# Halving the scatter of a mixture-of-experts block, with small moves in the steps before it

## The chip, the cores and the metric

One core of one Trainium2 chip. The metric is the device time of one launch in microseconds, the median of several runs. "The profiled execution" is one run recorded by the hardware profiler; its span reaches from the first to the last instruction. TensorE (PE) does the matmuls, VectorE (DVE), ScalarE (ACT) and GpSimd (POOL) the rest, SyncE (SP) and the other engines' queues start transfers.

## The reference

Four sequences of 1024 tokens with 512 channels (4096 tokens in all) go through one block:

```
h = layernorm(x) * (1 + ca) + sa                       # sa, ca, ga, sb, cb, gb from silu(c) @ wmod
x = x + ga * linear_attention(h)                        # relu(q), relu(k), 16 heads of 32, projection
h = layernorm(x) * (1 + cb) + sb
scores = sigmoid(h @ gate_w.T);  idx = top_2(scores + router_bias);  w = normalised scores of idx
routed = sum over the 2 chosen experts e:  w_e * (silu(h @ W1_e) * (h @ W3_e)) @ W2_e       # 8 experts, 352 wide
shared = (silu(h @ sw1) * (h @ sw3)) @ sw2                                                   # 704 wide
x = x + gb * (routed + shared)
```

## The kernel before, in words

Every fp32 operand of a large matmul is split in two fp16 parts, high and low, and a product is three matmuls (`split_matmul`, lines 86 to 88: high by high, high by low, low by high). Each engine runs its own hand-ordered program; semaphores join them. `TILES` is 32 (tiles of 128 tokens), `BT` is 8 tiles a sequence.

**Attention.** One loop over steps s does, for tile s, the layernorm, the projections and the sums of keys and values, and, for tile t = s - 9, `attend`, the output projection and the second layernorm; three tiles later come the router's `logits`. The attention part of a sequence needs that sequence's key-value product `vk` (`vk_high` on ScalarE, then `vk_low` on VectorE). The projection's weights are multiplied by the sequence's gate row on GpSimd (`wp_scale`), then split by ScalarE (`wp_high`) and VectorE (`wp_low`): `wp_turn(s)` says which piece in which step. Its last turn is at s = 32, the piece (3, 3). On GpSimd the order in a step is `shift2`, `deviation`, `add_bias`, `wp_scale`, `o_low`. On ScalarE `wp_high` comes after `vk_high` and before the first loads of expert weights and `activate(0)`.

**Shared expert.** From s = 32 on (TILES), two steps q of it go beside each attention step. A chunk is 256 tokens, 16 chunks of six steps: `up(q)` on TensorE, `activate(q)` and `high(q)` on ScalarE, `multiply(q)` and `low(q)` on VectorE; a chunk later in the order, `down(n)` for two tiles of 128 tokens. The sixth step is only 64 columns wide, so its high and low parts sit in the upper and lower 64 rows of one buffer, and the sixth pass of `down` is a 128-row matmul (line 1244) and a 64-row one (line 1245). `add_shared` adds the result to the output in HBM by an indirect transfer from GpSimd with an add. Meanwhile ScalarE and VectorE split the experts' weights, a piece in nearly every step.

**Routing.** After the attention loop (`TAIL_STEPS` is 24) the last `logits(31)` has to come before step 24: TensorE does it at the end of the loop, ScalarE copies it (`logits_out`), VectorE adds the halves (`sum_logits`), ScalarE waits for stores and for that sum and does the sigmoid. Then VectorE does between its steps `bias_scores` (24), `pick_first` (26), `pick_second` (27), `weigh` (28); TensorE counts ranks at step 30; VectorE does `add_runs`, `place`, `name_slots` (32 to 34), masks in steps 35 to 66, `name_tiles` (68) and `list_tokens` (69). The list names, for each of 71 slot tiles of 128 slots, the token and output row of each slot and the tile's expert. It lies where the last expert's weights will be, so ScalarE waits for it (`listed`) before that expert's first piece, at step 81.

**Expert stage.** For each of 71 slot tiles t: GpSimd gathers 128 rows of 2 KB (`gather`, line 422, six buffers), SyncE turns them by a transposing transfer, TensorE does `e_up(t)` (24 matmuls of 352 columns), VectorE and ScalarE form `a`, TensorE transposes it (`e_turn`, line 1323) and does `e_down(t)` (9 matmuls of 512 columns), and VectorE multiplies by a gate row into `y` (`e_out`, line 861, three buffers). TensorE's order is `e_turn(t-1)`, `e_up(t)`, `e_down(t-1)`; in `e_up` and in `e_down` it first reads the tile's expert number into a register. GpSimd's `scatter(t)` (line 428) adds `y` to the rows of the output in HBM. Since two tiles can hold the same token, and an adding transfer reads and then writes, scatter t waits until scatter t - 1 has landed; `e_out(t)` waits for scatter t - 3, to have its buffer free. GpSimd's order is `scatter(t)`, `gather(t + 7)`.

Of the kernel before, what the change touches and what calls it, by code (L numbers as in the profile page):

```python
# [7 lines left out]
I32 = mybir.dt.int32  # L8
U32 = mybir.dt.uint32
ALU = mybir.AluOpType  # L10
# [3 lines left out]
P = 128  # L14
# [39 lines left out]
PAIR_RING = 4  # L54
TURNS_FROM = TAIL_STEPS + 11
LISTED = 3
# [253 lines left out]
def gpsimd_program(nc, m, pool):  # L310
# [61 lines left out]
    for s in range(-3, TILES + TAIL):  # L372
        t = s - LAG
        if s == 0:
            step(pool.memset(m.ident[:, :], 0.0))
            step(pool.affine_select(out=m.ident[:, :], in_=m.ident[:, :], compare_op=ALU.not_equal, fill=1.0,
                                    base=0, pattern=[[-1, P]], channel_multiplier=1))
        if s == 1:
            step(pool.iota(m.row_no[:, :], [[P, TILES]], base=0, channel_multiplier=1))
        if s == 2:  # L380
            step(pool.memset(m.heads[:, :], VK_SCALE))
            step(pool.affine_select(out=m.heads[:, :], in_=m.heads[:, :], compare_op=ALU.is_ge, fill=0.0,
                                    base=0, pattern=[[-HEAD, 4]], channel_multiplier=1))
            step(pool.affine_select(out=m.heads[:, :], in_=m.heads[:, :], compare_op=ALU.is_ge, fill=0.0,
                                    base=HEAD - 1, pattern=[[HEAD, 4]], channel_multiplier=-1))
            step(pool.tensor_copy(m.head_mask[:, :].rearrange("p (h e) -> p h e", h=4),
                                  m.heads[:, :].unsqueeze(2).to_broadcast([P, 4, HEAD])))
        shift(s + 2)
        shift2(t - 2)
        deviation(s + 3)  # L390
        add_bias(t)
        for b, k in wp_turn(s):
            wp_scale(b, k)
        o_low(t)
        deviation2(t - 1)
        if s >= TILES:
            for q in range(STEPS_PER_SLOT * (s - TILES), STEPS_PER_SLOT * (s - TILES + 1)):
                if add_due(q):
                    add_shared(q // SH_TILES - 1)
# [25 lines left out]
    def scatter(t):  # L425
        pool.wait_ge(m.ey_ready, t + 1)
        at_least(pool, m.scattered, 16 * t)
        pool.indirect_dma_start(m.out, bass.IndirectOffsetOnAxis(ap=m.slot_row[:, t:t + 1], axis=0), m.y[:, t % Y_RING, :], None,  # L428
                                compute_op=ALU.add).then_inc(m.scattered, 16)

# [15 lines left out]
    for t in range(SLOT_TILES):  # L446
        scatter(t)
        gather(t + G_RING + 1)
    pool.wait_ge(m.scattered, 16 * SLOT_TILES)


def vector_program(nc, m, v):
# [342 lines left out]
    def list_tokens():  # L795
# [15 lines left out]
        step(v.tensor_tensor(m.rowf[:, :], m.rowf[:, :], m.tokenf[:, :], ALU.add))  # L811
        v.tensor_copy(m.slot_row[:, :], m.rowf[:, :]).then_inc(m.listed, 1)

    def name_tiles():
# [6 lines left out]

    beside = {TAIL_STEPS: (bias_scores,), TAIL_STEPS + 2: (pick_first,), TAIL_STEPS + 3: (pick_second,), TAIL_STEPS + 4: (weigh,),
              TAIL_STEPS + 8: (add_runs,), TAIL_STEPS + 9: (place,), TAIL_STEPS + 10: (name_slots,), LIST_STEP: (list_tokens,),
              LIST_STEP - 1: (name_tiles,)}
    sum_logits()
    for q in range(TAIL_STEPS, EARLY_STEPS):
# [30 lines left out]
    def e_out(t):  # L857
        v.wait_ge(m.ey_done, t + 1)
        v.wait_ge(m.gate_sum, (B - 1) * (t + 1))
        at_least(v, m.scattered, 16 * (t - Y_RING + 1))  # L860
        v.tensor_tensor(m.y[:, t % Y_RING, :], m.ps_ey[:, 0:C], m.gate_row[t % GW_RING][:, :], ALU.mult).then_inc(m.ey_ready, 1)  # L861
# [13 lines left out]
def scalar_program(nc, m, act):  # L875
# [139 lines left out]
    for s in range(-3, TILES + TAIL):  # L1015
# [42 lines left out]
        for j in m.mod_slots.get(s, ()):  # L1058
            act.wait_ge(m.mod_done, j + 1)
            act.activation(m.mod[:, j * C:(j + 1) * C], m.ps_mod[j], ACT.Copy).then_inc(m.mod_copied, 1)  # L1060
        for b, k in wp_turn(s):
            wp_high(b, k)
        if s == TILES:
            for p in range(W_RING - 1):
                w_load(p)
        if s >= TILES:
# [9 lines left out]
            convert_weights(q + 1)  # L1076
    logits_out(TILES - 1)
    for j in range(X2_RING):
        act.wait_ge(m.x2_stored[j], ring_uses(TILES, j, X2_RING))
    for j in range(2):  # L1080
        act.wait_ge(m.hl2_stored[j], ring_uses(TILES, j, 2))
    for j in range(H2T_RING):
        act.wait_ge(m.h2t_stored[j], ring_uses(TILES, j, H2T_RING))

    act.wait_ge(m.logits_ready, 1)
    act.activation(m.scores[:, :, :], m.logits[:, :, 0:E], ACT.Sigmoid).then_inc(m.scores_ready, 1)
    for q in range(TAIL_STEPS, EARLY_STEPS):
        activate(q)
        high(q - 1)
        if w_turn(q):  # L1090
            w_loads(w_turn(q)[0] + W_RING - 1)
        convert_weights(q)
# [29 lines left out]
def tensor_program(nc, m, pe):  # L1122
# [105 lines left out]
    def down(n):  # L1228
# [12 lines left out]
        for u in range(2):  # L1241
            tok = slice(u * P, (u + 1) * P)
            out = m.ps_sy[u][:, 0:C]
            nc.tensor.matmul(out, m.s_at[:, j, 0, tok], m.sh[:, 0, lo:lo + C], start=False, stop=False, skip_group_check=True)
            nc.tensor.matmul(out, m.s_at[0:SH_HALF, j, 0, tok], m.sh[0:SH_HALF, 1, lo:lo + C], start=False, stop=True, skip_group_check=True).then_inc(m.sy_done, 1)

# [11 lines left out]
    for s in range(TILES + TAIL):  # L1258
# [21 lines left out]
        if s >= TILES:  # L1280
# [3 lines left out]
            project_out(t - 1)  # L1284
        logits(t - 3)

    for q in range(TAIL_STEPS, EARLY_STEPS):
        up(q)
        if q == TAIL_STEPS + 6:
            pe.wait_ge(m.both_ready, 1)  # L1290
            pe.wait_ge(m.r_consts, 5)
            for part, lhs in ((0, m.before), (1, m.ones)):
                nc.tensor.matmul(m.ps_r[:, part, :], lhs[:, :], m.both[:, :, :].rearrange("p t e -> p (t e)"),
                                 start=True, stop=True).then_inc(m.ranks_done, 1)
# [11 lines left out]

    def e_up(t):
        expert = expert_of(t)
        pe.wait_ge(m.xt_loaded[t % G_RING], ring_use(t, G_RING))
# [15 lines left out]

    def e_down(t):
        expert = expert_of(t)
        pe.wait_ge(m.e_at_lo, t + 1)
# [10 lines left out]
    pe.wait_ge(m.consts, CONSTS)  # L1339
    e_up(0)  # L1340
    down(CHUNKS - 1)
    pe.wait_ge(m.a_padded, 1)
    for t in range(1, SLOT_TILES):
        e_turn(t - 1)
        e_up(t)
        if t == 1:
            pe.wait_ge(m.s_t1_done, 2 * CHUNKS)
        e_down(t - 1)
    e_turn(SLOT_TILES - 1)
    e_down(SLOT_TILES - 1)  # L1350


def place_buffers(nc, m):
# [16 lines left out]
    END = nc.sbuf_usable_end  # L1370
    KEPT = FIRST + 6400
    SHARED_AT = KEPT + 2 * SH_COLS * 2
# [9 lines left out]
    m.slot_token = sb("slot_token", [P, SLOT_TILES], I32)  # L1382
    m.slot_row = sb("slot_row", [P, SLOT_TILES], I32)
    m.row_no = sb("row_no", [P, TILES], I32)
# [130 lines left out]
def name_semaphores(m, sem):  # L1515
# [32 lines left out]
    m.gates_loaded, m.gate_first, m.gate_sum = sem("gates_loaded"), sem("gate_first"), sem("gate_sum")  # L1548
    m.scattered, m.spare_stored = sem("scattered"), sem("spare_stored")
    m.h1_done, m.h3_done, m.e_silu, m.e_act = sem("h1_done"), sem("h3_done"), sem("e_silu"), sem("e_act")  # L1550
# [94 lines left out]
```

## Time and profile before

| | |
|---|---|
| median of 3 runs | 1271.02 us (1267.22 to 1271.38) |
| profiled execution: time | 1265.33 us |
| its span | 1263.6 us |
| TensorE busy | 1202.6 us, 95% of the span |
| VectorE, ScalarE, GpSimd busy | 796.3, 416.6, 480.4 us |
| mean granted clock of TensorE | 0.991 |
| chain that ended last: scatters `out<-y,slot_row` | 25% of the span |
| expert stage | from about 808 us to the end |

The page of the profile gives busy times, their course in 40 slices, the transfer queues and the chain of work that ended last. Matmuls overlap in the array, so a matmul's duration is more than the distance to the next one; costs of TensorE are read from starts. The number in brackets behind an instruction is its engine's idle time before it and what ended that.

### The profile page before, as it was taken

To read this page: it belongs to the slowest core of one execution; us is meant where nothing else is said; L and a number is where in the kernel's file an instruction comes from. 1 tells how busy PE (TensorE), PEld (TensorE's weight loads), DVE (VectorE), ACT (ScalarE), POOL (GpSimd) and SP (SyncE) were. 2 spreads that over 40 slices of the span, in tenths; PEclk is the share of its full clock that TensorE was granted. 3 is DMA by queue.
4 is the path that set the end of the run, shared out by engine and by line. 5 is a ranking of instruction groups with operands and counts; after the bars stand their busy time and mean duration, and the time that the engine had idled before them with its cause. 6 is when DMAs were issued, how large, how long until landed. Compare 5 with 4: busy or idle time off the path is not lost.

```text
span 1263.6 us, 25262 instructions
## 1 busy us (share of the span) xinstructions
PE 1202.6 (95%) x9054; PEld 774.5 (61%) x9054; DVE 796.3 (63%) x1575; ACT 416.6 (33%) x873; POOL 480.4 (38%) x408
## 2 busy tenths in 40 slices
PE   7999999999998999999999999999999999999992
PEld 2646666666665666676776767566666555555551
DVE  6557778778765777476675643466666555555552
ACT  4324445444443333333332332222222222222220
POOL 2214566566554454311111102344443444344432
PEclk9999999999999999999999999999999999999996
DMA  7915698898788887453353443766766667777673
GB/s 232 234 44 150 169 220 207 214 231 202 190 209 188 221 201 177 105 131 94 93 141 84 103 128 77 164 126 126 126 126 126 125 126 121 131 126 122 118 108 46
DMA packets 253110, 185.01 MB, mean 146 GB/s; under 512 B 186480, under 2 KB 198768, under 8 KB 252988
## 3 DMA queue, kind: packets, MB, share of 16 engines
q1 hardware_dynamic: 217224, 114.14, 39.1%
q0 software_dynamic: 20512, 45.62, 20.9%
q10 hardware_dynamic: 15256, 23.62, 6.4%
q8 instruction: 80, 1.31, 0.4%
q14 instruction: 38, 0.31, 0.1%
HBM read 87.07 MB, written 52.49 MB: 110 GB/s over the span
## 4 chain that ended last, share of the span: by engine, by line
PE 37%; DMA 28%; issue 13%; POOL 11%; DVE 7%; ACT 2%; SPq 1%; POOLq 0%; ACTq 0%; DVEq 0%
DMA out<-y,slot_row 25%; PE ps_vs L86 3%; PE ps_vs L88 3%; PE ps_vs L87 3%; PE ps_vh L86 2%; PE ps_vh L88 2%; PE ps_vh L87 2%; POOL h L339 2%; PE ps_kh L86 2%; PE ps_kh L87 2%; PE ps_kh L88 2%; POOL xg L347 2%; POOL ol L352 2%; PE ps_qh L88 2%; PE ps_qh L86 2%
## 5 line engine op out<-in xcount | busy, mean ns | idle before, releaser
L428 POOL DMA_INDIRECT out<-y,slot_row x71 | 113.6, 1600 | 248.7 <-DMA out<-y,slot_row 223.1
L86 PE MATMUL ps_o<-w_all,xt 128*128 x568 | 177.8, 313 | 12.6 <-issue 12.3
L87 PE MATMUL ps_o<-w_all,xt 128*128 x568 | 177.6, 313 | 0.0
L88 PE MATMUL ps_o<-w_all,xt 128*128 x568 | 177.5, 313 | 0.0
L854 DVE SCALAR_TENSOR_TENSOR gate_row<-gate_rows,batch_weight,gate_row 128x512 f32<-128x512 f32 x213 | 158.9, 746 | 2.5
L366 POOL DMA_INDIRECT out<-s_sum,row_no x32 | 53.7, 1678 | 220.0 <-DVE s_sum L606 214.6
L861 DVE TENSOR_TENSOR y<-ps_vs,gate_row 128x512 f32<-128x512 f32 x71 | 49.1, 692 | 136.4 <-DMA out<-y,slot_row 118.0
L1105 ACT ACTIVATE at<-ps_y 128x384 f16<-128x384 f32 x71 | 34.9, 491 | 199.2 <-PE ps_y L1323 199.2
L328 POOL TENSOR_TENSOR h<-cen,rows_f 128x512 f32<-128x512 f32 x32 | 40.6, 1267 | 129.8 <-ACT cen L880 112.6
L1111 ACT ACTIVATE gate_row<-gate_rows,batch_weight 128x512 f32<-128x512 f32 x71 | 51.2, 722 | 115.2 <-DVE y L861 103.1
L86 PE MATMUL ps_qh<-ht,wqkv 128*128 128x128 f16 x512 | 87.4, 219 | 1.4 <-DVE wqkv L574 1.4
L87 PE MATMUL ps_qh<-ht,wqkv 128*128 128x128 f16 x512 | 87.4, 219 | 0.0
L88 PE MATMUL ps_qh<-ht,wqkv 128*128 128x128 f16 x512 | 87.4, 219 | 0.0
L422 POOL DMA_INDIRECT g<-h_d,slot_token x71 | 73.3, 1033 | 31.9 <-issue 21.1
L86 PE MATMUL ps_vs<-w_all,at 128*128 (+1 forms) x213 | 81.0, 380 | 4.4 <-DVE at L849 4.1
L86 PEld LDWEIGHTS ps_o<-w_all,xt 128*128 128x128 f16 x568 | 55.5, 98 | 46.2 <-issue 20.0
L581 DVE SCALAR_TENSOR_TENSOR s_act<-ps_vh,s_act 128x256 f32<-128x256 f32 x32 | 13.6, 423 | 111.4 <-ACT s_act L963 111.3
L88 PE MATMUL ps_vs<-w_all,at 128*128 (+1 forms) x213 | 80.6, 378 | 0.0
L87 PE MATMUL ps_vs<-w_all,at 128*128 (+1 forms) x213 | 80.6, 378 | 0.0
L87 PEld LDWEIGHTS ps_o<-w_all,xt 128*128 128x128 f16 x568 | 55.5, 98 | 27.3
L88 PEld LDWEIGHTS ps_o<-w_all,xt 128*128 128x128 f16 x568 | 55.6, 98 | 27.1
L87 PE MATMUL ps_kh<-s_ht,sh 128*128 128x256 f16 x256 | 70.4, 275 | 0.0
(247 smaller groups left out, 3321.3 us busy)
## 6 DMA issues: line engine op xcount, KB each, us to landing
w_stage<-in_w_d ACTq DMA_DIRECT2D x64, 176.0 KB, 2.6
xb<-in_x SPq DMA_DIRECT2D x32, 256.0 KB, 3.2
xr<-in_x SPq DMA_DIRECT2D x32, 256.0 KB, 3.7
out<-x SPq DMA_DIRECT2D x32, 256.0 KB, 3.4
h_d<-hl SPq DMA_DIRECT2D x32, 256.0 KB, 2.5
h2t_d<-h2t SPq DMA_DIRECT2D x32, 256.0 KB, 3.4
s_ht<-h2t_d SPq DMA_DIRECT2D x32, 256.0 KB, 3.5
sstage<-in_sh_flat SPq DMA_DIRECT2D x32, 136.0 KB, 3.2
```

What stands on the lines that cost most here:

```text
L86: nc.tensor.matmul(out, lh, rh, start=first, stop=False, skip_group_check=True)
L87: nc.tensor.matmul(out, lh, rl, start=False, stop=False, skip_group_check=True)
L88: return nc.tensor.matmul(out, ll, rh, start=False, stop=last, skip_group_check=True)
L328: pool.tensor_tensor(m.h[:, i % 2, :], m.cen[:, i % 2, :], m.rows_f[:, (i // BT) % 2, SA, :], ALU.add).then_inc(m.h_done, 1)
L339: pool.tensor_tensor(m.h2[:, t % 2, :], m.cen2[:, t % 2, :], m.rows_b[:, (t // BT) % 2, SB, :], ALU.add).then_inc(m.h2_done, 1)
L366: pool.indirect_dma_start(m.out, bass.IndirectOffsetOnAxis(ap=m.row_no[:, t:t + 1], axis=0), m.s_sum[:, u, :], None, compute_op=ALU.add).t ...
L422: pool.indirect_dma_start(m.g[r][:, :], None, m.h2_d, bass.IndirectOffsetOnAxis(ap=m.slot_token[:, t:t + 1], axis=0)).then_inc(m.gathered[ ...
L428: pool.indirect_dma_start(m.out, bass.IndirectOffsetOnAxis(ap=m.slot_row[:, t:t + 1], axis=0), m.y[:, t % Y_RING, :], None, compute_op=ALU ...
L854: v.scalar_tensor_tensor(out=row, in0=m.gate_rows[:, b, :], scalar=m.batch_weight[:, b, t:t + 1], in1=row, op0=ALU.mult, op1=ALU.add).then ...
L861: v.tensor_tensor(m.y[:, t % Y_RING, :], m.ps_ey[:, 0:C], m.gate_row[t % GW_RING][:, :], ALU.mult).then_inc(m.ey_ready, 1)
L1105: act.activation(m.at[:, t % 2, 0, :, :], m.ps_a[:, :, :], ACT.Copy).then_inc(m.e_at_hi, 1)
L1111: act.activation(m.gate_row[t % GW_RING][:, :], m.gate_rows[:, 0, :], ACT.Copy, scale=m.batch_weight[:, 0, t:t + 1]).then_inc(m.gate_first, 1)
```

## The change

It does five things.

- The scatter of a slot tile is made of two transfers, one for each half of the 512 columns. The output is seen as rows of 256 columns, so `slot_row` holds two lists (2 x row, and 2 x row + 1), and each half has its own semaphore, on which it waits for the same half of the tile before. `e_out` waits for both.
- The last turn of the projection's weights (s = 32) is moved: on GpSimd behind `o_low`, on ScalarE to the end of the step.
- The sixth pass of `down` uses all 128 rows in its second matmul (the low activations by the low weights are added by it, a product that was left out before).
- `logits(31)` moves behind `up(25)`, `logits_out(31)` to ScalarE's step 26, `sum_logits` to VectorE's step 26, the sigmoid to ScalarE's step 27; the choice follows at 28 to 30, the ranks at 32 (`RANK_STEP`), `add_runs`, `place` and `name_slots` at 38 to 40, the masks from 41, the list at 75.
- TensorE reads the next tile's expert number before `e_turn`, and keeps it for `e_down`.

```diff
-TURNS_FROM = TAIL_STEPS + 11
+RANK_STEP = TAIL_STEPS + 8
+TURNS_FROM = RANK_STEP + 9
...
         add_bias(t)
-        for b, k in wp_turn(s):
-            wp_scale(b, k)
+        if s < TILES:
+            for b, k in wp_turn(s):
+                wp_scale(b, k)
         o_low(t)
+        if s >= TILES:
+            for b, k in wp_turn(s):
+                wp_scale(b, k)
...
     def scatter(t):
         pool.wait_ge(m.ey_ready, t + 1)
-        at_least(pool, m.scattered, 16 * t)
-        pool.indirect_dma_start(m.out, bass.IndirectOffsetOnAxis(ap=m.slot_row[:, t:t + 1], axis=0), m.y[:, t % Y_RING, :], None,
-                                compute_op=ALU.add).then_inc(m.scattered, 16)
+        for half in range(2):
+            at_least(pool, m.scattered[half], 16 * t)
+            pool.indirect_dma_start(m.out.rearrange("t (h c) -> (t h) c", h=2), bass.IndirectOffsetOnAxis(ap=m.slot_row[:, half, t:t + 1], axis=0),
+                                    m.y[:, t % Y_RING, half * C // 2:(half + 1) * C // 2], None,
+                                    compute_op=ALU.add).then_inc(m.scattered[half], 16)
...
-        v.tensor_copy(m.slot_row[:, :], m.rowf[:, :]).then_inc(m.listed, 1)
+        step(v.tensor_scalar(m.slot_row[:, 0, :], m.rowf[:, :], 2.0, None, ALU.mult))
+        v.tensor_scalar(m.slot_row[:, 1, :], m.rowf[:, :], 2.0, 1.0, ALU.mult, ALU.add).then_inc(m.listed, 1)
...
-    beside = {TAIL_STEPS: (bias_scores,), TAIL_STEPS + 2: (pick_first,), TAIL_STEPS + 3: (pick_second,), TAIL_STEPS + 4: (weigh,),
-              TAIL_STEPS + 8: (add_runs,), TAIL_STEPS + 9: (place,), TAIL_STEPS + 10: (name_slots,), LIST_STEP: (list_tokens,),
-              LIST_STEP - 1: (name_tiles,)}
-    sum_logits()
+    beside = {TAIL_STEPS + 2: (sum_logits,), TAIL_STEPS + 4: (bias_scores, pick_first), TAIL_STEPS + 5: (pick_second,),
+              TAIL_STEPS + 6: (weigh,), RANK_STEP + 6: (add_runs,), RANK_STEP + 7: (place,), RANK_STEP + 8: (name_slots,),
+              LIST_STEP: (list_tokens,), LIST_STEP - 1: (name_tiles,)}
...
     def e_out(t):
-        at_least(v, m.scattered, 16 * (t - Y_RING + 1))
+        for half in range(2):
+            at_least(v, m.scattered[half], 16 * (t - Y_RING + 1))
...
-        for b, k in wp_turn(s):
-            wp_high(b, k)
+        if s < TILES:
+            for b, k in wp_turn(s):
+                wp_high(b, k)
         if s == TILES:
             for p in range(W_RING - 1):
                 w_load(p)
...
             convert_weights(q + 1)
+            for b, k in wp_turn(s):
+                wp_high(b, k)
...
     for q in range(TAIL_STEPS, EARLY_STEPS):
         activate(q)
         high(q - 1)
+        if q == TAIL_STEPS + 2:
+            logits_out(TILES - 1)
+        if q == TAIL_STEPS + 3:
+            score()
...
-            nc.tensor.matmul(out, m.s_at[0:SH_HALF, j, 0, tok], m.sh[0:SH_HALF, 1, lo:lo + C], start=False, stop=True, skip_group_check=True).then_inc(m.sy_done, 1)
+            nc.tensor.matmul(out, m.s_at[:, j, 0, tok], m.sh[:, 1, lo:lo + C], start=False, stop=True, skip_group_check=True).then_inc(m.sy_done, 1)
...
-        logits(t - 3)
+        if t - 3 < TILES - 1:
+            logits(t - 3)
     for q in range(TAIL_STEPS, EARLY_STEPS):
         up(q)
-        if q == TAIL_STEPS + 6:
+        if q == TAIL_STEPS + 1:
+            logits(TILES - 1)
+        if q == RANK_STEP:
...
     for t in range(1, SLOT_TILES):
+        following = expert_of(t)
         e_turn(t - 1)
-        e_up(t)
+        e_up(t, following)
-        e_down(t - 1)
+        e_down(t - 1, expert)
+        expert = following
```

## Rows read from the trace of the kernel before

**Rows 1.** Windows (stretch: length, busy time of each engine, PEclk granted, DMA share, GB/s).

```profile
920.00:960.00 40.00, 40.00 (x247) 24.46 (x246) 25.92 (x41) 10.87 (x21) 16.96 (x13) 1.00 0.66 125
```

**Rows 2.** Waits, 830 to 1255 us (who, for whom: us in total, times, longest).

```profile
POOL out L428 <- DMA out<-y,slot_row: 213.7, 62, 5.9
DVE y L861 <- DMA out<-y,slot_row: 118.0, 46, 3.9
```

**Rows 3.** Chain that ended last, 1000 to 1030 us (start, us, what).

```profile
1010.79 5.50 DMA out<-y,slot_row
...
1016.34 0.71 issue
```

**Rows 4.** All instructions and transfers that read `slot_row` (durations min/median/max).

```profile
L428 POOL DMA_INDIRECT out<-y,slot_row x71: 1543/1567/2039, 815.6 to 1255.6; - x71
...
DMA to landing us min/median/max: 4.5/5.5/6.8
```

**Rows 5.** Timeline of TensorE, expert stage (start, us, instruction, idle before).

```profile
818.14 0.49 PE L1323 MATMUL ps_y<-ident,a 128*128 128x128 f32 x3
...
970.35 0.49 PE L1323 MATMUL ps_y<-ident,a 128*128 128x128 f32 x3
...
1237.99 0.49 PE L1323 MATMUL ps_y<-ident,a 128*128 128x128 f32 x3
...
1241.65 0.38 PE L88 MATMUL ps_vs<-w_all,at 96*128 x1
```

**Rows 6.** Timeline of GpSimd, expert stage.

```profile
885.53 1.00 POOL L422 DMA_INDIRECT g<-h_d,slot_token  x1 [0.30 <-issue]
...
1255.64 1.54 POOL L428 DMA_INDIRECT out<-y,slot_row  x1 [4.00 <-DMA out<-y,slot_row]
```

**Rows 7.** Transfer queues, 830 to 980 us (packets, MB, share of 16 engines).

```profile
q0 software_dynamic: 5349, 12.53, 44.9%
q1 hardware_dynamic: 24985, 6.20, 23.4%
```

**Rows 8.** Transfer queues, 1251.5 to 1255.5 us: one scatter, nothing beside it.

```profile
q0 software_dynamic: 144, 0.26, 54.8%
...
out<-y,slot_row POOLq DMA_INDIRECT x1, 4.8
```

**Rows 9.** GB/s in 40 slices, 866 to 872 us.

```profile
GB/s 0 0 0 0 0 0 0 0 96 123 0 14 14 41 68 96 191 218 205 205 195 176 237 203 200 162 227 288 292 424 287 218 410 246 382 28 0 0 0 0
```

**Rows 10.** Timeline of TensorE, end of one `down` and the next `up`.

```profile
432.65 0.38 PE L88 MATMUL ps_vs<-sh,s_at 128*128 128x512 f16 x1
432.87 0.38 PE L1244 MATMUL ps_vs<-sh,s_at 128*128 128x512 f16 x1
...
434.14 0.28 PE L86 MATMUL ps_vh<-s_ht,sh 128*128 128x256 f16 x1
```

**Rows 11.** Timeline of TensorE (first row) and ScalarE, step 32.

```profile
393.52 0.22 PE L86 MATMUL ps_o<-vk,qt 128*128 128x132 f16 x1
...
398.83 0.63 ACT L943 ACTIVATE wproj<-wp_raw 128x512 f16<-128x512 f32 x1 [3.09 <-POOL wp_raw L359]
...
400.19 0.38 ACT L963 ACTIVATE s_act<-ps_kh 128x256 f32<-128x256 f32 x1 [0.73 <-issue]
```

**Rows 12.** Timeline of TensorE, steps 32 and 33.

```profile
402.29 0.17 PE L1203 MATMUL ps_o<-gate,h2t 128*128 128x16 f16 x1 [2.70 <-issue]
...
407.91 0.22 PE L86 MATMUL ps_o<-vk,qt 128*128 128x132 f16 x1 [2.64 <-DVE vk L508]
```

**Rows 13.** Timeline of TensorE: the last logits, and a `down` during the choosing.

```profile
518.90 0.18 PE L1203 MATMUL ps_o<-gate,h2t 128*128 128x16 f16 x1 [2.81 <-DMA h2t<-hl]
...
548.50 0.39 PE L86 MATMUL ps_vs<-sh,s_at 128*128 128x512 f16 x1 [1.63 <-DVE s_at L593]
```

**Rows 14.** Timeline of ScalarE: the sigmoid's table load; a second follows it.

```profile
521.66 1.28 ACT L1086 ACT_TABLE_LOAD   x1 [2.18 <-DMA h2t_d<-h2t]
```

**Rows 15.** Timeline of VectorE: one step of choosing (the next starts 0.46 later).

```profile
538.75 0.42 DVE L732 SCALAR_TENSOR_TENSOR sel<-choice,sel 128x256 f32<-128x256 f32 x1
```

More of the change, by code:

```diff
@@ L448, in gpsimd_program @@
         gather(t + G_RING + 1)
-    pool.wait_ge(m.scattered, 16 * SLOT_TILES)
+    for j in range(2):
+        pool.wait_ge(m.scattered[j], 16 * SLOT_TILES)
 def vector_program(nc, m, v):
@@ L1076, in scalar_program, with score @@
             convert_weights(q + 1)
[L1077 to L1086, printed above, removed]
+            for b, k in wp_turn(s):
+                wp_high(b, k)
+    def score():
+        for j in range(X2_RING):
+            act.wait_ge(m.x2_stored[j], ring_uses(TILES, j, X2_RING))
+        for j in range(2):
+            act.wait_ge(m.hl2_stored[j], ring_uses(TILES, j, 2))
+        for j in range(H2T_RING):
+            act.wait_ge(m.h2t_stored[j], ring_uses(TILES, j, H2T_RING))
+        act.wait_ge(m.logits_ready, 1)
+        act.activation(m.scores[:, :, :], m.logits[:, :, 0:E], ACT.Sigmoid).then_inc(m.scores_ready, 1)
     for q in range(TAIL_STEPS, EARLY_STEPS):
@@ L1305, in expert_of, with e_up @@
         return pe.value_load(m.eid[0:1, t:t + 1], min_val=0, max_val=E - 1)
-    def e_up(t):
-        expert = expert_of(t)
+    def e_up(t, expert):
         pe.wait_ge(m.xt_loaded[t % G_RING], ring_use(t, G_RING))
@@ L1324, in e_turn, with e_down @@
         mm.then_inc(m.at_done, 1)
-    def e_down(t):
-        expert = expert_of(t)
+    def e_down(t, expert):
         pe.wait_ge(m.e_at_lo, t + 1)
@@ L1339, in tensor_program @@
     pe.wait_ge(m.consts, CONSTS)
-    e_up(0)
+    expert = expert_of(0)
+    e_up(0, expert)
     down(CHUNKS - 1)
@@ L1343, in tensor_program @@
     for t in range(1, SLOT_TILES):
+        following = expert_of(t)
         e_turn(t - 1)
-        e_up(t)
+        e_up(t, following)
         if t == 1:
             pe.wait_ge(m.s_t1_done, 2 * CHUNKS)
-        e_down(t - 1)
+        e_down(t - 1, expert)
+        expert = following
     e_turn(SLOT_TILES - 1)
-    e_down(SLOT_TILES - 1)
+    e_down(SLOT_TILES - 1, expert)
 def place_buffers(nc, m):
@@ L1370, in place_buffers @@
     END = nc.sbuf_usable_end
-    KEPT = FIRST + 6400
+    KEPT = FIRST + 6976
     SHARED_AT = KEPT + 2 * SH_COLS * 2
@@ L1382, in place_buffers @@
     m.slot_token = sb("slot_token", [P, SLOT_TILES], I32)
-    m.slot_row = sb("slot_row", [P, SLOT_TILES], I32)
+    m.slot_row = sb("slot_row", [P, 2, SLOT_TILES], I32)
     m.row_no = sb("row_no", [P, TILES], I32)
@@ L1548, in name_semaphores @@
     m.gates_loaded, m.gate_first, m.gate_sum = sem("gates_loaded"), sem("gate_first"), sem("gate_sum")
-    m.scattered, m.spare_stored = sem("scattered"), sem("spare_stored")
+    m.scattered, m.spare_stored = ring("scattered", 2), sem("spare_stored")
     m.h1_done, m.h3_done, m.e_silu, m.e_act = sem("h1_done"), sem("h3_done"), sem("e_silu"), sem("e_act")
```

## The prediction

> **What bounds the kernel now.** I read the windows first. In the last third (the expert stage) TensorE is busy nearly throughout at granted clock 1.00, the 2.4 GHz level [rows 1], so by busy share the stage would seem TensorE's. The waits say otherwise: from 830 to 1255 us GpSimd's scatter waited 213.7 us for the scatter before it, and VectorE's `y` 118.0 us for a scatter [rows 2]. The chain shows the link: a landing of 5.50 us, 0.71 us of issue, the next scatter [rows 3]. 71 scatters start from 815.6 to 1255.6 us, 440.0/70 = 6.286 us apart, and take 5.5 us (4.5 to 6.8) to land [rows 4]. TensorE's own need shows before the backlog has filled the three `y` buffers: transposes at 818.14 and, 26 tiles later, at 970.35, 5.854 us a tile. Its last transposes are at 1237.99, its last matmul at 1241.65 [rows 5]; the last scatter starts at 1255.64 [rows 6], 14 us behind TensorE. So the expert stage is bound by the serial scatter; the stages before it by TensorE, but for a few gaps [rows 12, 13].
>
> **The change, part by part.**
>
> 1. **Scatter by halves.** Removed: 71 scatters of 128 rows of 2 KB. Added: 142 of 128 rows of 1 KB, each waiting only for its own half of the tile before. No 1 KB scatter is in the trace. A whole one, alone on the queues, lands in 4.8 us, and its packets take 54.8% of 16 engines in 4 us, 35.1 us, or 0.27 us for each of 128 rows [rows 8]. So 35.1/16 = 2.2 us of the 4.8 is data and 2.6 is not (1.54 of it the instruction, rows as before [rows 6]). A 1 KB packet costs from 0.135 us (all by bytes) to 0.27 us (all by packet; I see no reason for more, or for less than half). I take 0.19, near the middle, since no row is nearer to either end. Alone, a half then lands in 2.6 + 128 x 0.19/16 = 4.1 us; beside the gather and the transposes I add the 0.7 by which 5.5 exceeds 4.8: 4.8 us, bounds 4.4 and 5.5. The link is that plus 0.75: 5.55 us (5.1 to 6.25). A half that lands within 5.1 us leaves TensorE's 5.854 as the bound.
>  GpSimd: descriptor work should go by rows, so 1.57 us twice [rows 4], the gather 1.00, and 0.30 ahead of each [rows 6]: 5.04 us, 5.5 if one wait costs 0.75 instead of 0.30; by bytes it would be 3.5. All under 5.854. Behind a waiting second half stands the gather for a tile seven later, with some 35 us to spare.
>  Transfer engines: the software queue's 44.9% and the transposes' 23.4% of 16 x 150 us are 45 + 23 = 68 us for each of 24 tiles [rows 7]. The halves add 256 x 0.19 - 35 = 14: 82 of the 93.7 us in 16 x 5.854, a share of 0.88.
>  So TensorE sets the pace. 68 tiles at 5.854 from 818.14 put the last transposes at 1216.2 instead of 1237.99. The last matmul starts 3.7 later, 1219.9, and `y` is ready at 1220.9. The first half before the last starts at 1217.4 (its tile's matmuls ended at 1216.2), so the last first half starts at 1217.4 + 4.8 + 0.75 = 1222.9, the second 1.87 later, and lands 4.1 after that, at 1228.9. The span ended 1263.6 - 1255.64 - 4.8 = 3.2 us after the last landing: 1232.1. **Stage: 31.5 us less.**
> 2. **Step 32** (the one `wp_turn` with s >= TILES). `up(0)` was over at 393.5; ScalarE sat idle 3.09 us for GpSimd's product, converted it (0.63 us) at 398.83 and did the first `activate` only at 400.19 [rows 11]. VectorE stands behind that, and TensorE twice: 2.70 us before the logits, 2.64 before `attend` [rows 12]. With the turn moved behind, the wait and the conversion leave the path: 3.7 us. The first gap goes, the second stays in part. GpSimd's product now follows `o_low`; `wproj` is needed two steps on, which hides it. **3.7 us**; 0 if something else holds `activate`, 5.3 (both gaps) at most.
> 3. **Full sixth down pass.** Matmuls of 512 columns start 0.22 us apart (432.65, 432.87); the four passes with the 64-row ones between take 1.27 us (432.87 to 434.14) [rows 10], 0.39 more than four at 0.22. The columns stay, so full rows should give 0.22. 15 of 16 downs lie where TensorE is the bound, the last in a wait for gate rows: 5.9 us, a little of it absorbed in gaps that follow the first ones. **5.5 us**, 0 to 5.9.
> 4. **Last logits and the routing two steps later.** Removed: TensorE's 2.81 us for the last transposed tile, 3.0 with its issue. Next late was a `down` that waited 1.63 us [rows 13] for VectorE, then behind some 20 steps of choosing and weighing of up to 0.45 us [rows 15]. Now ScalarE does the sigmoid between two activations; two table loads of 1.28 us [rows 14] make it 1.2 us late once. VectorE does bias and first choice (7 x 0.45 = 3.2 us) before that `down`'s fifth block, by my count of its queue 0.1 to 0.3 us late; the weighing (some 3.3 us) falls behind it. 3.0 + 1.6 - 0.2: **4.4 us**; 0.9 if the later start pushes the `down` by a further 2.1. Ranks and list come two and six steps later, at the same places between the downs (69 and 75 are both 3 mod 6); ScalarE needs the list at step 81, for the last expert's first weights, so six steps of slack are left: 0.
> 5. **Expert number read earlier**: no gap stood before `e_up` at 5.854 a tile, so 0. One more column operation in the list: 0.2 us beside TensorE.
>
> **Sum** against the profiled execution (span 1263.6, time 1265.33): 31.5 + 3.7 + 5.5 + 4.4 = 45.1 less, 1220.2. That execution lies 5.7 us under the median of the runs shown, 1271.02; against the median it is **1225.9 us**.
>
> **The rivals** (13.6 us is the sum of parts 2 to 4).
> - **Fixed landing.** A half saves only its bytes. The highest rate of a slice here is 424 GB/s [rows 9]; 131 KB at that is 0.3 us, so 5.2 us to land and a link of 5.95. Against it: 0.27 us a packet is far slower than that rate. Last link at 815.6 + 70 x 5.95 = 1232.1, + 1.87 + 4.5 + 3.2 = 1241.7, stage 21.9 less: **1235.5 us**.
>  The Trainium skill, DMA: Bandwidth & Descriptors (Anatomy of one DMA, SWDGE path), gives about 2.0 us fixed plus bytes/436e3; by it a half saves 0.30 us too, which speaks against the full gain. The trace has only one size of scatter and can't tell.
> - **GpSimd binds.** Both waits unmet at 0.75 and descriptor work of 1.6 (up to 2.0 is seen [rows 4]): 2 x 1.6 + 2 x 0.75 + 1.0 + 0.3 = 6.0. Against it: the second half's wait is met while the first is issued. (6.286 - 6.0) x 70 - 1.9 for the second half = 18.1: **1239.3 us**.
> - **Pair, not halves.** The second half queues behind the first and both land when a whole one did; then the split doesn't do what it says. Stage 2 us longer: **1259.4 us**.
> - **Slower: transfer engines full.** At 0.27 us a packet, 256 x 0.27 + 33 = 102 us of engine time a tile; at a usable share of 0.9 (my choice) 7.1 us. (7.1 - 6.286) x 70 - 13.6 = +43: **1314 us**. It turns slower from 6.286 + 13.6/70 = 6.48 us a tile, 0.235 us a packet. For it: these packets are slow for their bytes. Against: an engine has several in hand, so part of 0.27 is overlap.
>
> **How the numbers follow.** Forecast 0.57 (own range 1217 to 1232, from the bounds of parts 2 to 4); fixed landing 0.16; GpSimd 0.10; pair 0.08; transfer engines 0.09, 0.02 of it near no change. The range leaves out the last two: 1217 to 1246. A change within 0.3% is about what a measurement can't tell from none. Faster 0.91, same 0.02, slower 0.07.
>
> **What would show it.** Right: transposes 5.85 us apart to the end, `y` waiting for no scatter, halves landing within 5.1 us, the last matmul near 1206; the first `activate` of step 32 near 396.5; down passes 0.22 apart throughout; no gap at the last logits. Wrong: halves landing in 5.5 us, scatters again first of the waits, or a transfer share near 1. The price of a 1 KB packet is the largest risk.

## The result and the profile after

| | before | changed |
|---|---|---|
| median of 4 runs each, one chip | 1269.12 us | 1219.33 us |
| lowest to highest | 1264.63 to 1271.38 | 1218.78 to 1220.49 |
| profiled execution: span | 1263.6 us | 1217.5 us |
| expert stage, from one tile's transposes to the next | 6.286 us (scatter starts) | 5.853 us |
| GpSimd busy | 480.4 us | 603.5 us |

The ratio is 0.9613 (95% interval 0.9582 to 0.9644): 3.9% faster. The waits of the expert stage in the changed kernel, 830 to 1200 us (who, for whom: us in total, times, longest), against [rows 2]:

```profile
ACT at L1121 <- PE ps_y L1341: 226.7, 63, 3.6
...
POOL out L434 <- DVE y L870: 60.3, 64, 2.6
DVE y L870 <- PE ps_vs L89: 47.9, 63, 0.8
```

The 213.7 us and 118.0 us that two engines spent behind a landing scatter are gone. In this execution GpSimd waits for `y`, and `y` for TensorE. Everything that read `slot_row` in the whole span says how little is left of the waits for a transfer, against [rows 4]:

```profile
L434 POOL DMA_INDIRECT out<-y,slot_row x142: 1544/1558/1765, 800.6 to 1210.0; - x142
...
POOL out L434: 4.0, 7
```

The instruction takes 1.56 us for 128 rows of 1 KB in this execution, as it took 1.57 for 128 rows of 2 KB; the second execution below shows 1.9. TensorE's timeline, against [rows 5]:

```profile
798.73 0.49 PE L1341 MATMUL ps_y<-ident,a 128*128 128x128 f32 x3
...
1202.61 0.49 PE L1341 MATMUL ps_y<-ident,a 128*128 128x128 f32 x3
...
1206.10 0.38 PE L89 MATMUL ps_vs<-w_all,at 96*128 x1
```

69 tiles between the first two rows: 403.88/69 = 5.853 us, to the last tile. GpSimd's timeline shows how near it is to being next, against [rows 6]:

```profile
998.91 1.57 POOL L434 DMA_INDIRECT out<-y,slot_row  x1 [0.85 <-DVE y L870]
1000.79 1.55 POOL L434 DMA_INDIRECT out<-y,slot_row  x1 [0.31 <-issue]
1002.64 1.28 POOL L427 DMA_INDIRECT g<-h_d,slot_token  x1 [0.30 <-issue]
```

Of 5.85 us it waits 0.85 for `y`, and 0.3 of those are its own issue. This margin of 0.55 us is that of one execution; the changed kernel again (below) has hardly any. The windows of the same 300 us, changed kernel (columns as in [rows 1]):

```profile
850.00:1150.00 300.00, 300.00 (x1845) 183.45 (x1843) 196.97 (x308) 80.81 (x153) 224.48 (x155) 1.00 0.84 136
```

and the kernel before:

```profile
850.00:1150.00 300.00, 291.64 (x1770) 175.41 (x1769) 181.60 (x293) 76.27 (x146) 125.02 (x95) 1.00 0.69 126
```

TensorE's idle time was only 8.4 us of 300 by this count, 2.8%, while it did 4% fewer matmuls (1770 against 1845), and over the whole stage a tile took 7% longer at the scatter. Since a matmul's record is longer than the distance to the next, the busy share hides a part of a stretched sequence; the starts don't. The transfer share went from 0.69 to 0.84.

**Where the 46.1 us of span went.** To the transposes of the second tile 13.2 us (811.93 before, 798.73 now): that is the small moves. From there to the last transposes 22.2 us (426.1 before, 403.9 now): the pace. From these to the end 10.7 us (25.6 before, 14.9 now): no queue of scatters is left. The chain shows the end, 1200 to 1218 us (start, us, what):

```profile
1202.81 0.70 DVE y L870
1203.51 0.27 issue
1203.77 3.63 DMA out<-y,slot_row
...
1207.44 0.71 issue
1208.15 1.54 POOL out L434
```

A half lands in 3.63 us with only the other half of its tile beside it, where the whole one took 4.8 [rows 8].

### The profile page after: what moved, and what is told of

It is laid out like the page before. It is cut to its first block, busy times and chain, and to the rows that moved or that the text cites. A ratio compares the mean times of both kernels' runs of the same rounds, so it can differ in the third digit from the quotient of the medians.

```text
span 1217.5 us, 25189 instructions
## 1 busy us (share of the span) xinstructions
PE 1188.3 (98%) x9054; PEld 777.0 (64%) x9054; DVE 804.4 (66%) x1576; ACT 417.4 (34%) x873; POOL 603.5 (50%) x479
## 4 chain that ended last, share of the span: by engine, by line
PE 88%; DVE 3%; DMA 3%; issue 2%; ACT 1%; SPq 1%; POOL 1%; ACTq 0%; DVEq 0%; POOLq 0%
PE ps_o L87 7%; PE ps_o L89 7%; PE ps_o L88 7%; PE ps_vs L87 6%; PE ps_vs L88 6%; PE ps_vs L89 6%; PE ps_kh L87 4%; PE ps_vh L87 4%; PE ps_vh L89 4%; PE ps_vh L88 4%; PE ps_kh L89 4%; PE ps_kh L88 4%; PE ps_qh L87 4%; PE ps_qh L88 4%; PE ps_qh L89 4%
## 5 line engine op out<-in xcount | busy, mean ns | idle before, releaser
L434 POOL DMA_INDIRECT out<-y,slot_row x142 | 221.5, 1560 | 94.7 <-DVE y L870 70.6
L427 POOL DMA_INDIRECT g<-h_d,slot_token x71 | 87.3, 1230 | 31.9 <-issue 19.2
L852 DVE SCALAR_TENSOR_TENSOR a<-ps_o,a 128x352 f32<-128x352 f32 x71 | 37.3, 525 | 73.9 <-PE ps_o L89 69.5
L589 DVE SCALAR_TENSOR_TENSOR s_act<-ps_vh,s_act 128x256 f32<-128x256 f32 x32 | 13.6, 423 | 103.8 <-ACT s_act L972 103.7
```

The lines of the kernel that those rows point to most:

```text
L427: pool.indirect_dma_start(m.g[r][:, :], None, m.h2_d, bass.IndirectOffsetOnAxis(ap=m.slot_token[:, t:t + 1], axis=0)).then_inc(m.gathered[ ...
L434: pool.indirect_dma_start(m.out.rearrange("t (h c) -> (t h) c", h=2), bass.IndirectOffsetOnAxis(ap=m.slot_row[:, half, t:t + 1], axis=0), ...
L589: v.scalar_tensor_tensor(out=m.s_act[:, q % 2, :], in0=m.ps_h[j % 3][:, 1, :], scalar=1.0 / SCALE, in1=m.s_act[:, q % 2, :], op0=ALU.mult, ...
L852: v.scalar_tensor_tensor(out=m.a[:, t % 2, 0:INTER], in0=m.ps_h3[:, 0:INTER], scalar=1.0 / SCALE, in1=m.a[:, t % 2, 0:INTER], op0=ALU.mult ...
```

## The experiments

All kernels below are the changed one with one edit, except the fifth. Times are medians of 4 runs where no other is said, each beside 7 runs of the kernel before on the same chip.

**The changed kernel again.** No edit.

> The changed kernel once more, on the chip of the next three. Both theories: its runs lie within 0.15% of each other (1218.8 to 1220.5 so far), while the kernel before scatters over 0.5% (1264.6 to 1271.4). Theory A: the spread of before is that of its scatter landings (4.5 to 6.8 us, 71 in series), so it comes back only where the serial scatter is the bound. Theory B: it is the chip's or the run's, then this kernel spreads over some 6 us too on a fourth to eighth run.

1219.33 us (1218.00 to 1221.08), ratio 0.9624 (0.9580 to 0.9668). The kernel before gave 1265.95 beside it (1263.19 to 1273.80). The spread of 0.25% against 0.8% speaks for theory A; the expected 0.15% was too tight.

The profiled execution of this run shows what the first one didn't. GpSimd, and what read `slot_row`:

```profile
900.42 2.02 POOL L434 DMA_INDIRECT out<-y,slot_row  x1 [0.30 <-issue]
902.75 1.91 POOL L434 DMA_INDIRECT out<-y,slot_row  x1 [0.30 <-issue]
904.96 1.00 POOL L427 DMA_INDIRECT g<-h_d,slot_token  x1 [0.30 <-DMA out<-y,slot_row]
906.27 2.02 POOL L434 DMA_INDIRECT out<-y,slot_row  x1 [0.30 <-issue]
```

```profile
DMA to landing us min/median/max: 3.5/4.8/6.2
```

2.02 + 1.91 + 1.00 + 3 x 0.30 = 5.83 us: GpSimd is full at a tile's 5.85, and the halves land in 4.8 us. TensorE's transposes are 5.853 us apart all the same (798.44 to 1202.32, 69 tiles), and the time is the same. Of the eight profiled executions with the halves on two chains and TensorE at 5.85, four look like this one (this run and those of the last weights' turn back, the expert number late and the two more moves) and four like the first. Why the instruction takes 1.9 to 2.0 us in some was not looked into and stays open.

**The last weights' turn back.**

```diff
+        for b, k in wp_turn(s):        # GpSimd: before o_low; ScalarE: before the first loads and activate(0)
```

> Of the changed kernel only the move of the last turn of the projection's weights (step 32) is undone. Theory A (the wait stood on the path of TensorE): ScalarE's first activate is again some 3.7 us later after the vk conversion, the logits of that step wait again 2.7 us on TensorE, and the time is 3 to 4 us more, 1222.5 to 1223.5. Theory B (the later gaps of TensorE absorb it, or vk's low part was the last to be late anyway): within 1 us of 1219.3.

1223.03 us (1221.45 to 1223.56): 3.7 more than the changed kernel on the same chip, as in the next two. ScalarE in the changed kernel, at step 32, against [rows 11]:

```profile
394.71 0.64 ACT L957 ACTIVATE vk<-vk_tmp 128x528 f16<-128x528 f32 x1
394.72 1.30 ACTq L991 DMA_DIRECT2D w_stage<-in_w_d  x3
396.07 0.38 ACT L972 ACTIVATE s_act<-ps_kh 128x256 f32<-128x256 f32 x1 [0.71 <-issue]
```

With the turn back the rows are again those of before (product awaited until 398.83, `activate` at 400.19). Theory A.

**The sixth pass with 64 rows.**

```diff
-            nc.tensor.matmul(out, m.s_at[:, j, 0, tok], m.sh[:, 1, lo:lo + C], ...
+            nc.tensor.matmul(out, m.s_at[0:SH_HALF, j, 0, tok], m.sh[0:SH_HALF, 1, lo:lo + C], ...
```

> Of the changed kernel only the full sixth pass is undone: the second matmul has 64 rows again (the product of low activations and low weights is left out, as in the kernel before). Theory A: each of the four starts around it takes 0.32 us instead of 0.22, 0.4 us a down, and 15 of 16 downs lie on the path: 5.5 to 6.1 us more, 1224.8 to 1225.4. Theory B: the 0.1 us is absorbed where TensorE waits for other engines: under 2 us more.

1224.46 us (1223.62 to 1224.73): 5.1 more by the medians, 5.5 and 5.8 by the span of the profiled execution against the two of the changed kernel. TensorE in the changed kernel, against [rows 10]:

```profile
429.51 0.38 PE L1260 MATMUL ps_vs<-sh,s_at 128*128 128x512 f16 x1
429.72 0.38 PE L1261 MATMUL ps_vs<-sh,s_at 128*128 128x512 f16 x1
429.94 0.38 PE L1260 MATMUL ps_vs<-sh,s_at 128*128 128x512 f16 x1
430.15 0.38 PE L1261 MATMUL ps_vs<-sh,s_at 128*128 128x512 f16 x1
430.37 0.27 PE L87 MATMUL ps_vh<-s_ht,sh 128*128 128x256 f16 x1
```

Four passes take 0.86 us instead of 1.27. With 64 rows back:

```profile
428.82 0.39 PE L1261 MATMUL ps_vs<-sh,s_at 64*128 64x512 f16 x1
429.13 0.39 PE L1260 MATMUL ps_vs<-sh,s_at 128*128 128x512 f16 x1
429.46 0.39 PE L1261 MATMUL ps_vs<-sh,s_at 64*128 64x512 f16 x1
429.78 0.28 PE L87 MATMUL ps_vh<-s_ht,sh 128*128 128x256 f16 x1
```

Each start after a change of the row count is 0.31 to 0.33 us behind the one before. Twice the rows, and the work is faster. Theory A, a little under its lower end. But this execution was lucky elsewhere: its TensorE did not fall to the lower clock before its end, which cost the changed kernel 1.7 us (last section). The changed kernel with the expert number late has the same program up to the expert stage and no fall either. From the logits at 390 us to the first transposes it takes 399.15 us (391.16 to 790.31), this kernel 406.28 (390.54 to 796.82). So like with like the full rows are worth 7.1 us, 0.45 for each of 16 downs.

**Logits and routing back.**

```diff
-RANK_STEP = TAIL_STEPS + 8
+RANK_STEP = TAIL_STEPS + 6        # and logits(31), its copy, the sum and the sigmoid before step 24, choice in 24 to 28
```

> Of the changed kernel only the later logits and routing are undone (logits before step 24, choice in steps 24 to 28, ranks at 30, list at 69). Theory A: TensorE waits again 2.8 us at the last logits and some 1.6 us in the down of step 30, where the changed kernel waits 0.8: 3.5 to 4.5 us more, 1222.8 to 1223.8. Theory B: only the stall moves, the time is within 1 us of 1219.3.

1223.64 us (1222.88 to 1225.61): 4.3 more, theory A. TensorE, with the logits back:

```profile
513.37 0.19 PE L1218 MATMUL ps_o<-gate,h2t 128*128 128x16 f16 x1 [2.79 <-DMA h2t<-hl]
...
543.80 0.39 PE L87 MATMUL ps_vs<-sh,s_at 128*128 128x512 f16 x1 [1.63 <-DVE s_at L601]
```

They are [rows 13] again. In the changed kernel the first is gone and the second is shorter:

```profile
539.54 0.39 PE L87 MATMUL ps_vs<-sh,s_at 128*128 128x512 f16 x1 [0.61 <-DVE s_at L601]
```

**Only the scatter.** The kernel before with the scatter by halves and nothing else.

> The kernel before with the scatter by halves alone (without the small moves, the expert numbers read where they were). Theory A (the serial scatter was the bound, TensorE's 5.854 us a tile is the next): transposes 5.85 us apart to the end, no wait of y for a scatter, 32 to 33 us less than the profiled execution of before, and 35 to 37 less than its median: about 1232 to 1234. Theory B (the early reading of the expert numbers has a part in it): gaps of some 0.3 to 0.8 us ahead of the first matmul of a tile remain, and the time is 1240 or more.

1235.14 us (1232.08 to 1236.68), ratio 0.9758 (0.9684 to 0.9831), against 1264.53 for before beside it (1258.55 to 1275.84): 29.4 less. TensorE's transposes of the third and the last tile:

```profile
817.19 0.49 PE L1328 MATMUL ps_y<-ident,a 128*128 128x128 f32 x3
...
1215.32 0.49 PE L1328 MATMUL ps_y<-ident,a 128*128 128x128 f32 x3
```

398.13/68 = 5.855 us: the full pace without the early expert numbers, so theory A on the mechanism. The time is a little over its range, and 15.8 over the changed kernel on another chip, where the span of the profiled execution is 12.8 over and the three undone parts add up to 13.1. The runs that would show what the slower of the four did have no trace; this stays open. The four spread over 4.6 us, though no chain of landings bounds this kernel.

**Whole scatter, small moves kept.**

```diff
-        for half in range(2):
-            at_least(pool, m.scattered[half], 16 * t)
+        at_least(pool, m.scattered, 16 * t)        # one indirect transfer of whole rows, as before
```

> The changed kernel with the whole scatter back and the small moves kept. Theory A: parts add up; the expert stage is again 6.29 us a tile, the time is the median of before less the 13 us of the small moves, 1255 to 1257, with the runs spread over 0.3 to 0.5% again. Theory B (the early expert number gives the stage something by itself): below 1253.

1250.97 us (1247.15 to 1253.43), ratio 0.9885 (0.9810 to 0.9960). By the number alone this is theory B's (below 1253). But both numbers were reckoned from 1269; against 1264.53, the kernel before beside it, it is 13.6 less, as theory A says (by the ratio's interval 5 to 24), and the pace below is that of before, so the early expert number gives the stage nothing. The stage is serial again:

```profile
L433 POOL DMA_INDIRECT out<-y,slot_row x71: 1543/1567/2039, 799.5 to 1237.7; - x71
...
DMA out<-y,slot_row: 221.2, 65
```

438.2/70 = 6.26 us a tile, 221.2 us of waits for a landing.

**Expert number late.**

```diff
-        following = expert_of(t)
...
-        e_up(t, following)
+        e_up(t)                        # reads the number itself, and e_down(t - 1) too
```

> Of the changed kernel only the early reading of the expert numbers is undone. Theory A: at 5.85 us a tile the reading is hidden in every tile but the second (6.21 instead of 5.85 in the trace of before): 0.4 us more, 1219.7. Theory B: it is exposed wherever TensorE's queue runs dry, 0.2 us and more in many of 71 tiles: 1225 or more.

1219.00 us (1218.56 to 1219.74): no difference from 1219.33. The second tile shows the 0.36 us of theory A (transposes at 797.56 and 803.77, 6.21 apart), all after it 5.85. In the time it can't be seen: this execution had no fall of the clock before its end, where the changed kernel's had one.

**First half waits for both.** The transfers are as small as in the changed kernel, but the chain is one again.

```diff
         for half in range(2):
-            at_least(pool, m.scattered[half], 16 * t)
+            for other in range(2 - 2 * half):
+                at_least(pool, m.scattered[other], 16 * t)
```

> The changed kernel, but the first half of a scatter waits until both halves of the tile before have landed, so the transfers are as small as in the changed kernel and the chain is one again. Theory A (the gain is in the two chains side by side; a half lands in some 4.0 to 4.5 us beside the rest): a link is 1.87 + 4.0 to 4.5 + 0.75 = 6.6 to 7.1 us, the stage is bound by it, 20 to 60 us over the kernel before less the small moves: 1280 to 1315. Theory B (the gain is that small transfers land early enough even in one chain): up to 5.85 us a link, no loss, 1219 to 1222.

1293.22 us (1289.49 to 1294.86), ratio 1.0217 (1.0140 to 1.0294): 2.2% slower than before. What read `slot_row`:

```profile
L435 POOL DMA_INDIRECT out<-y,slot_row x142: 1544/1562/2083, 799.5 to 1280.1; - x142
...
DMA to landing us min/median/max: 3.6/4.0/5.4
```

The last pair starts at 1278.3, so a tile takes 478.8/70 = 6.84 us; 1.85 + 4.0 + 0.75 = 6.6 is the link, the rest is the landings over 4.0. Halving alone makes a chain worse: it shortens a landing by 1.4 us (5.4 with the whole scatter, 4.0 here) and adds a 1.85 us issue. What pays is that two chains run side by side. Theory A.

**Second scatter of whole rows.** Two scatters a tile on two chains, both of 2 KB rows, the second to a spare buffer in HBM.

```diff
-        for half in range(2):
+        for half, target in enumerate((m.out, m.spare_out)):        # both whole rows of y
```

> Two scatters a tile, each of whole rows of 2 KB, on two chains: one to the output, one to a spare buffer in HBM (it doubles the added bytes; the output is as it should be). Theory A (a packet's price goes mostly by its bytes, 0.27 us at 2 KB and 0.16 at 1 KB): engine time 256 x 0.27 + 33 = 102 us a tile, a share near 1 at 5.85, so 6.5 to 7.1 us a tile and 1265 to 1310 in all. Theory B (a price by packet: 1 KB costs about the same): little differs from the changed kernel, 1219 to 1225.

1264.36 us (one run; before 1267.85, median of 7): between the two numbers' ranges, just under theory A's. What read `slot_row`, and the queues (830 to 980 us, columns as in [rows 7]):

```profile
L434 POOL DMA_INDIRECT out<-y,slot_row x71: 1543/1567/2053, 800.5 to 1251.9; - x71
...
POOL out L434: 59.9, 37
POOL spare_out L434: 42.9, 42
...
DMA to landing us min/median/max: 4.8/5.6/9.3
```

```profile
q0 software_dynamic: 8725, 18.60, 75.8%
q1 hardware_dynamic: 24288, 6.03, 29.7%
```

451.4/70 = 6.45 us a tile, the two queues' shares together 105% of the engines. That the transfer engines are the bound at 102/16 = 6.4 us is not shown by this. A sum of packet times over 100% means that packets overlap on an engine, so it doesn't say how full the engines are. And each chain is one of whole rows again, whose link was 6.29 us in the kernel before: a landing of 5.6 here and 0.75 are 6.35, and scatters waited for a landing 79 times. For the same reason theory B's 1219 to 1225 could not have come about, whatever a packet costs. What the run does show is a limit: with 256 packets of 2 KB a tile, the 102 us of engine time of the slower rival, a tile takes 6.45 us and not 7.1, so even at its worst price the change would have ended near the time of before.

**Quarters.**

```diff
-        for half in range(2):
+        for half in range(4):        # 128 columns, four lists, four semaphores
```

> The scatter in four quarters of 128 columns, each with its own semaphore. Theory A (descriptor work on GpSimd goes by rows, 1.55 us however short the row): GpSimd needs 4 x 1.86 + 1.55 = 9.0 us a tile, becomes the bound, and the time is about 1219 + 70 x 3.15 = 1440. Theory B (it goes by bytes): four of 0.8 us, GpSimd at 5.9 us a tile, 1219 to 1230.

1432.6 us (one run), theory A. What read `slot_row`, and GpSimd near the end:

```profile
L434 POOL DMA_INDIRECT out<-y,slot_row x284: 1546/1570/2070, 804.3 to 1423.2; - x142
...
DMA to landing us min/median/max: 3.2/3.3/4.9
```

```profile
1417.69 1.55 POOL L434 DMA_INDIRECT out<-y,slot_row  x1 [0.30 <-issue]
```

The instruction's time goes by rows, not bytes: a median of 1.56 to 1.57 us at 2 KB, 1 KB (first execution) and 512 B. (1417.7 - 804.3)/70 = 8.76 us a tile, GpSimd's 4 x 1.86 + 1.3. By the same sum thirds would take 6.9 us, an estimate, so of the equal splits only halves fit under 5.85.

**Two more moves.**

```diff
+        if s == TILES:
+            vk_low(s // BT - 1)        # before multiply(0) instead of at the end of the step
...
-    for t in range(4):
+    for t in range(2):                 # the gate rows are loaded after two transposes, not four
         turn_g(t)
```

> The changed kernel with two more moves: at step 32 VectorE does the low part of vk before the shared expert's first multiply instead of at the end of the step, and SyncE loads the gate rows before the third and fourth transposes instead of behind them. Theory A: the waits of TensorE at 401.8 us (2.67) and at 795 us (1.70) go: 3.5 to 4.4 us less, 1215 to 1216. Theory B: what stands behind each is late by as much (the gathers' transposes share the queue with the gate rows): within 1 us of 1219.3.

1215.79 us (1215.32 to 1216.42), ratio 0.9591 (0.9575 to 0.9607) against 1267.85: 3.5 us less than the changed kernel (on another chip), the fastest here, and the number of theory A. The second move gave its 1.7 (the first transposes that were 7.56 us apart are 5.85). Up to the first transposes it is 1.6 us ahead, but not by the wait alone:

```profile
402.68 0.22 PE L87 MATMUL ps_o<-vk,qt 128*128 128x132 f16 x1 [0.44 <-issue]
...
415.36 0.39 PE L87 MATMUL ps_y<-wproj,ot 128*128 128x512 f16 x1 [1.79 <-DMA ot<-ol]
```

`attend` waits 0.44 us instead of 2.51, and the output projection two steps on waits 1.79 for its transposed tile, which takes back nearly all of it. The 1.6 us are about what the clock gives, which does not fall here (last section). From the logits at 390 us to the first transposes this kernel takes 399.06 us (390.53 to 789.59); the one with the expert number late, which has no fall either, took 399.15. So like with like the first move gives 0.1 us, and the recorded mechanism of theory A holds for the second move only. Whether the shorter wait is what kept the clock up is open.

## Why the prediction was right, point by point

**The bound.** Right, and shown from both sides: with the whole scatter kept the stage stays at 6.26 us a tile, with the halves alone it goes to TensorE's 5.85.

**The half's price.** I took 0.19 us a packet between 0.135 and 0.27. Alone at the end of the changed kernel, 1209.5 to 1214 us, two halves show:

```profile
q0 software_dynamic: 288, 0.26, 50.2%
```

0.502 x 4.5 x 16/256 = 0.141 us a row of 1 KB, against 0.27 for 2 KB. The price goes by bytes, nearly at the lower bound. A landing took 3.63 us near the end where I had 4.1 alone, and 4.0 (median) beside the gather in the kernel with one chain where I had 4.8. So the term was over-sized for a half alone, and in the first execution the margin was larger: the transfer share is 0.84 (I had 0.88) and hardly a half was waited for. In the second execution of the same kernel it was not over-sized: the halves landed in 4.8 us, the share was 0.87, and a scatter waited for a landing 19 times, 14.6 us in all. The result didn't depend on it, since TensorE's pace was the bound in both; only the end did, which was 1.0 us shorter than in my sum (14.9 against 15.9).

**The sum.** Stage 32.9 against 31.5 forecast (pace 22.2 against 21.8, with the second tile's 0.36 that I had put at 0; end 10.7 against 9.7); step 32 3.7 against 3.7; sixth pass 5.1 to 5.5 against 5.5; logits and routing 4.3 against 4.4. The down of step 30 waited 0.61 us, not 0.1 to 0.3, and the rest of that part was right. The sixth pass was under-sized: 7.1 us like with like, where I had 0.39 for each of 15 downs and 5.9 as the most. Three undone parts add to 13.1 by the medians and the stretch before the expert stage lost 13.2, an agreement in part by luck, since the fall of the clock is in some of these executions and not in others. From the logits at 390 us to the first transposes, executions with one fall each give 2.6 for step 32 (403.42 against 400.85) and 4.0 for the logits (404.84); with the 7.1 that is 13.7, and the kernel before lost 13.4 there (414.28). So they are additive within some 0.3 us. In all 46.1 of span against 45.1.

**The number itself.** The sum against the profiled execution gave 1220.2, and 1219.33 was measured. I then added 5.7 us, the distance of that execution to the median of three runs, to come to 1225.9. That step failed, and it is nearly all of the 6.6 us of error. The three runs shown lay high (1271.02; medians with more runs were 1269.12, 1265.95, 1264.53 and 1267.85), and the kernel before spreads over 1258.6 to 1275.8 us in all its runs. The changed kernel's eight runs lie within 3.1 us, and with the whole scatter back it is 6.3 us again. I read this so: a chain of 71 landings of 4.5 to 6.8 us carries each one's luck into the total, the change removes the chain, and an offset that comes from the part being removed should not have been carried over. It is argued, not shown: the kernel with the scatter by halves alone has no such chain at the bound and spread over 4.6 us, on the chip where the one with the expert number late spread over 1.2.

That 1219.33 lies in the stated range of 1217 to 1232 is partly luck. The best ends of parts 2 and 3 (5.3 and 5.9 instead of 3.7 and 5.5) take 2.0 us off 1225.9, to 1223.9; no bound of parts 2 to 4 leads to 1217.

**The rivals.** Fixed landing fell: a half saves 1.2 us, not 0.3. By the fit in the Trainium skill, DMA: Bandwidth & Descriptors (Anatomy of one DMA, SWDGE path), 131 KB are worth an estimated 0.30 us. The traces don't agree for adding scatters, and the measurement decides at 1.17 (4.8 to 3.63). GpSimd binds: fell by the time, but narrowly. The descriptor work of 2.0 us that I had seen only as a longest case was the common one in four executions, where GpSimd was full at 5.83 of 5.85 us; at quarters the rival is true. Pair, not halves: true of a kernel that waits for both, not of this one. Transfer engines: fell, since a 1 KB packet costs 0.14 us and not 0.27. How full the engines can be was not settled; twice the added bytes gave 6.45 us a tile where a usable share of 0.9 would give 7.1.

## What to carry to other kernels

Where a serial chain of read-add-write transfers is the bound, cut it into chains that touch different bytes and need not wait for each other; making the pieces smaller without a second chain makes it slower. The limit of the cut is the engine that issues the scatters: here 1.86 us a piece of 128 rows, whatever its bytes, against a tile's 5.85, and up to 2.3 us a piece in other executions of the same kernel, with which two pieces just fit. One execution's idle time is no margin; look at a second one. And take the forecast from the profiled execution as it stands, unless the offset to the median comes from something that the change leaves in place.

## What was not expected of the hardware

After the waits at step 32 TensorE is slow for a while, in some executions. The window of 405 to 408 us (columns as in [rows 1]) in the changed kernel:

```profile
405.00:408.00 3.00, 3.00 (x21) 2.21 (x19) 1.87 (x6) 1.29 (x3) 1.19 (x1) 0.55 0.61 133
```

with 64 rows in the sixth pass:

```profile
405.00:408.00 3.00, 3.00 (x35) 2.74 (x33) 1.91 (x6) 1.30 (x3) 0.99 (x1) 1.00 0.60 140
```

with the two more moves:

```profile
405.00:408.00 3.00, 3.00 (x21) 1.83 (x19) 1.87 (x6) 1.30 (x3) 1.61 (x2) 1.00 0.57 131
```

and of the kernel before:

```profile
408.00:410.00 2.00, 2.00 (x17) 1.73 (x17) 1.35 (x3) 0.61 (x1) 0.06 (x1) 0.53 0.75 221
```

The granted clock falls to the 1.2 GHz level for 3 to 4 us; in the kernel before, the 24 matmuls of 256 columns from 409.03 to 412.76 took 3.7 us instead of 2.5. From one step's logits to the next the changed kernel takes 13.06 us (399.05 to 412.11) and the one with the expert number late, without the fall, 11.39 (399.89 to 411.28), with the same program up to there. So a fall costs 1.7 us.

It doesn't follow from the length of the gap before it. Where `attend` waited 2.5 us at this place, three profiled executions show the fall (the changed kernel twice, quarters) and six don't (64 rows, logits back, whole scatter, expert number late, first half waits for both, second whole scatter). With the 2.70 us wait of the kernel before, all three show it (before, turn back, only the scatter). With a wait of 0.44 us, in the kernel with the two more moves, it did not come. The wait of 2.81 us at 518.90 in the kernel before [rows 13] passed without one; with the logits back, the fall came there, at the wait of 2.79. What decides stays open. The prediction had no term for it. It needed none, because the executions of before and after show one fall each; but 1.7 us is a good part of the differences of 3.5 to 5.5 us by which the small moves were judged, so they were worth a second profiled execution.
